# A GNN layer with a routed expert FFN on one core: exact tile counts and the gate's share inside the product in the experts, a 32-bit gate product and constants made earlier in the route

## The reference, cut to what matters

```
x = x + gnn(layernorm(x))            # segment sum over edges, two products, batch norm
h = layernorm(x)
logits = h @ gate_w + gate_b         # (12500, 8)
idx = argmax(softmax(logits)); prb = the softmax at idx
pos = cumsum(one_hot(idx)) of the own expert - 1;  kept = pos < 1954
buf[idx, pos] = h                    # 8 experts x 1954 slots
y = relu(buf @ w1[e] + b1[e]) @ w2[e] + b2[e]      # 256 -> 1024 -> 256
x = x + nan_to_num(y[idx, pos] * prb * kept)
```

## Time and profile before

| | us |
|---|---|
| the profiled execution, device time | 3170.35 |
| its span, first to last instruction | 3168.4 |
| median of the three runs | 3167.32 |
| norm and edge stages in the span | 0 to 2327 |
| route | 2327 to 2543 |
| experts | 2543 to 3168 |

### The profile page before, as it was taken

The page is one execution under the profiler, slowest core; times in us unless marked ns, Lnnn a source line. Parts: engine busy times, 40 slices in busy tenths (PEclk is TensorE's granted clock), DMA queues, the critical chain, the costliest instruction groups (busy, mean ns, idle before and its releaser), DMA issues. The chain is left out here.

```text
span 3168.4 us, 33068 instructions
## 1 busy us (share of the span) xinstructions
PE 1799.3 (57%) x9168; PEld 1062.1 (34%) x9169; DVE 1478.5 (47%) x4301; ACT 693.1 (22%) x1092; POOL 1709.5 (54%) x1690
## 2 busy tenths in 40 slices
PE   0154444455445555554754555564665568989995
PEld 0022222222223222222322222232345445566664
DVE  8765511643225313531252122212348757776885
ACT  6600000000010001000100101010046654636642
POOL 0366664655646565554655344435315556767874
PEclk9976667677767777776777777877766589999997
DMA  7533354334633354343423332212246432222220
GB/s 245 190 104 105 117 183 143 105 89 129 206 96 97 118 195 132 91 127 118 152 85 122 107 123 67 59 50 79 53 144 205 144 94 74 71 86 74 78 83 18
DMA packets 201528, 361.15 MB, mean 114 GB/s; under 512 B 62117, under 2 KB 125947, under 8 KB 201334
## 3 DMA queue, kind: packets, MB, share of 16 engines
q0 software_dynamic: 69152, 185.00, 19.6%
q1 hardware_dynamic: 130038, 172.60, 16.8%
q10 hardware_dynamic: 2144, 1.05, 0.1%
HBM read 291.08 MB, written 71.92 MB: 115 GB/s over the span
## 5 line engine op out<-in xcount | busy, mean ns | idle before, releaser
L773 POOL DMA_INDIRECT halves<-table,halves x1240 | 1186.5, 957 | 1006.4 <-issue 365.6
L850 PE MATMUL e_sums<-halves 128*128 128x256 f16 x1920 | 337.9, 348 | 392.5 <-issue 241.0
L1033 DVE SCALAR_TENSOR_TENSOR nodes<-e_sums,above,nodes 128x256 f32 (+1 forms) x161 | 77.5, 481 | 984.2 <-remote 465.9
L850 PEld LDWEIGHTS e_sums<-halves 128*128 128x128 f16 x1920 | 231.4, 123 | 512.2 <-issue 428.5
L956 ACT ACTIVATE e_hT<-e_up 128x1024 f32<-128x1024 f32 (+1 forms) x25 | 25.1, 1005 | 1511.2 <-remote 1146.8
L1720 POOL TENSOR_TENSOR x_midl<-x_midf,x_midh 128x512 f16<-128x512 f32 x200 | 298.5, 1517 | 103.6 <-ACT x_midh L1854 98.7
L907 PE MATMUL e_up<-e_hT,W1s 128*128 128x512 f32 (+1 forms) x400 | 230.6, 737 | 214.3 <-ACT e_hT L956 117.3
L888 PE MATMUL e_tally<-w1f,counts 128*128 128x512 f16 x490 | 163.1, 477 | 278.9 <-DMA w1f<-table 196.5
L1097 DVE TENSOR_TENSOR counts<-counts,e_tally 128x490 f32 x220 | 160.2, 728 | 243.5 <-PE e_tally L878 124.7
L1810 PE MATMUL x_down<-halves,x_midh 128*128 128x256 f16 x1472 | 251.2, 278 | 19.9 <-DVE x_yb L1947 13.2
L1786 PE MATMUL x_up<-x_xTh,halves 128*128 128x512 f16 (+1 forms) x800 | 231.9, 369 | 3.4 <-ACT x_midh L1854 1.9
(11 more groups left out here) (219 smaller groups left out, 2742.0 us busy)
## 6 DMA issues: line engine op xcount, KB each, us to landing
w1f<-table SPq DMA_DIRECT2D x120, 512.0 KB
halves<-table,halves POOLq DMA_INDIRECT x1240
slot_rows<-halves SPq DMA_DIRECT2D x64, 268.0 KB
x_row<-slot_rows SPq DMA_DIRECT2D x32, 536.0 KB, 7.2
table<-halves SPq DMA_DIRECT2D x25, 512.0 KB, 3.0
counts<-in_x SPq DMA_DIRECT2D x24, 512.0 KB, 5.1
r_xin<-in_x SPq DMA_DIRECT2D x24, 512.0 KB
out<-r_row SPq DMA_DIRECT2D x24, 512.0 KB, 3.3
```

The lines of the kernel that those rows point to most:

```text
L773: pool.indirect_dma_start(got[:, r, t, :], None, table.rearrange("p h d -> (p h) d"), bass.IndirectOffsetOnAxis(ap=idx[:, r, t:t + 1], axi ...
L850: ins = nc.tensor.matmul(sums[:, place, 0:D], hot[:, place, t, :], got[:, r, t, half * D:(half + 1) * D], start=(t == 0 and half == 0), st ...
```

## The change

In the experts: `branch` takes a number of steps, by which `work` gets a tile count. PE has the exact count (1 to 4); ACT's `hidden`, POOL's `low_hidden` and DVE's `finish` have 2 or 4; POOL's `scatter` issues for 2 or 4 tiles. ACT, at the end of `hidden`, writes `b2p` = b2 * prob in four activations of 128x256. DVE has a new function `product` ahead of `finish`: four operations, one per tile, y = down * share + b2p, where `share` = prob * scale is one more small operation in `meta`. They take the place of `yb` and `y`. The memset of `res` covers all of it. PE's `product_down` waits for `product` of the step before.

In the route: `xTh` and `xTl` become one 32-bit `xT`, written by ACT alone; DVE's `low_columns` and the split of the gate's weights go; `gate` is 8 matmuls of 32-bit operands. `seen` is kept for each of the four tiles, so DVE's reduction `more` goes, and `counts` has three matmuls more. The node number in the row is written by ACT in `columns` and no longer by DVE in `route`; POOL waits for it. The four constants are made by POOL at the end of the edge stage, in memory that the edge stage used for zeros.

```diff
@@ stage_edges, at the end of POOL's program
+                pool.wait_ge(s_zeroed, 16 * ZEROS)
+                pool.wait_ge(s_blank, NU * COUNT_ZEROS)
+                nc.gpsimd.memset(fixed.ones[:, :], 1.0).then_inc(s_ones, 1)
+                nc.gpsimd.iota(fixed.rev[:, :], pattern=[[-1, NX]], base=NX, channel_multiplier=0,
+                               allow_small_or_imprecise_dtypes=True)
+                nc.gpsimd.iota(fixed.node1[:, :], pattern=[[P, NB]], base=1, channel_multiplier=1,
+                               allow_small_or_imprecise_dtypes=True)
+                pool.wait_ge(s_ones, 1)
+                nc.gpsimd.affine_select(out=fixed.tri[:, :], in_=fixed.ones[:, :], compare_op=ALU.is_ge, fill=0.0,
+                                        base=0, pattern=[[1, P]], channel_multiplier=-1)
@@ stage_route, tensor
             def gate(q, j, rnd):
-                pe.wait_ge(s_xlo, q + 1)
+                pe.wait_ge(s_xT, q + 1)
                 ...
                 for t in range(QT):
-                    passes = [(x, w, k) for k in range(DK) for x, w in ((xTh, gwh), (xTh, gwl), (xTl, gwh))]
-                    for n, (x, w, k) in enumerate(passes):
-                        ins = nc.tensor.matmul(logit[:, t, :], x[:, k, t * P:(t + 1) * P], w[:, k, :],
-                                               start=(n == 0), stop=(n == len(passes) - 1))
+                    for k in range(DK):
+                        ins = nc.tensor.matmul(logit[:, t, :], xT[:, k, t * P:(t + 1) * P], gw[:, k, :],
+                                               start=(k == 0), stop=(k == DK - 1))
+            def earlier(width, place, last):
+                for t in range(QT):
+                    ins = nc.tensor.matmul(count[:, 0:width, :], ones[:, :],
+                                           seen[:, place, t, :].unsqueeze(1).broadcast_to((P, width, NX)),
+                                           start=(last and t == 0), stop=(last and t == QT - 1))
+                return ins
@@ stage_route, scalar
-                nc.scalar.activation(xTh[:, :, :], back[:, :, :], ACT.Identity, scale=X_SCALE).then_inc(s_xT, 1)
+                nc.scalar.activation(xT[:, :, :], back[:, :, :], ACT.Identity).then_inc(s_xT, 1)
+                nc.scalar.activation(row[:, j, :, D + 2], node1[:, at(q, QT)], ACT.Identity).then_inc(s_col, 1)
@@ stage_route, vector
-            def low_columns(q, j, rnd):
-                dve.wait_ge(s_xT, q + 1)
-                nc.vector.scalar_tensor_tensor(out=xTl[:, :, :], in0=back[:, :, :], scalar=X_SCALE,
-                                               in1=xTh[:, :, :], op0=ALU.mult, op1=ALU.subtract
-                                               ).then_inc(s_xlo, 1)
...
-                picked(q, 7, nc.vector.tensor_reduce(more[:, :], hot[:, :, :].rearrange("p t e -> p e t"), AX.X, ALU.add))
-                picked(q, 7)
-                nc.vector.tensor_tensor(seen[:, (j + 1) % R5, :], seen[:, j, :], more[:, :],
+                nc.vector.tensor_tensor(seen[:, (j + 1) % R5, :, :], seen[:, j, :, :], hot[:, :, :],
                                         ALU.add).then_inc(s_hot, 1)
-            walk(dve, [(low_columns, 3), (add, 1), (route, 3), (norm, 1)], NQ, R5)
+            walk(dve, [(add, 1), (route, 3), (norm, 1)], NQ, R5)
@@ stage_experts
-            def branch(own, j, work, skip, narrow=False):
+            def branch(own, j, work, skip, steps=1):
...
+                def between(low, high):
+                    if high - low == 1:
+                        return work(high * QT // steps) if high else skip()
+                    middle = (low + high) // 2
+                    with engine.If(used > base + middle * QT // steps):
+                        between(middle, high)
+                    with engine.Else():
+                        between(low, middle)
+
+                between(-1, steps)
@@ stage_experts, gpsimd
-                            nc.gpsimd.tensor_tensor(midl[:, j % 2, c, :], midf[:, c % MB, :], midh[:, j % 2, c, :],
+                            nc.gpsimd.tensor_tensor(midl[:, j % 2, c, cols], midf[:, c % MB, cols], midh[:, j % 2, c, cols],
                                                     ALU.subtract).then_inc(s_mlo, 1)
...
-                nc.gpsimd.memset(res[0:16, 0, 0, :], 0.0).then_inc(s_still, 1)
+                nc.gpsimd.memset(res[:, :, :, :], 0.0).then_inc(s_still, 1)
@@ stage_experts, tensor
-                            pe.wait_ge(s_yv, s * 7 - 6)
+                            pe.wait_ge(s_yv, (s - 1) * GUARD + 1)
@@ stage_experts, scalar, at the end of hidden's work
+                        act.wait_ge(s_w, expert(j, rnd) * 64 + 16)
+                        act.wait_ge(s_meta, s * META + META)
+                        if not (isinstance(s, int) and s < 2):
+                            act.wait_ge(s_yv, (s - 2) * GUARD + 1)
+                        for t in range(QT):
+                            ins = nc.scalar.activation(b2p[:, j % 2, t, :], b2s[:, h, :], ACT.Identity,
+                                                       scale=prob[:, j, t:t + 1])
+                        ins.then_inc(s_b2p, 1)
@@ stage_experts, vector
+                def product(s, j, rnd):
+                    def work(tiles):
+                        dve.wait_ge(s_down, s + 1)
+                        dve.wait_ge(s_b2p, s + 1)
+                        ...
+                        for t in range(tiles):
+                            ins = nc.vector.scalar_tensor_tensor(out=y[:, t, :], in0=down[:, t, :], scalar=share[:, j, t:t + 1],
+                                                                 in1=b2p[:, j % 2, t, :], op0=ALU.mult, op1=ALU.add)
+                        ins.then_inc(s_yv, 1)
...
-                        then(1, nc.vector.scalar_tensor_tensor(
-                            out=yb[:, :, :], in0=down[:, :, :], scalar=1.0 / (MID_SCALE * W_SCALE),
-                            in1=b2s[:, j // SG, :].unsqueeze(1).broadcast_to((P, QT, D)), op0=ALU.mult, op1=ALU.add))
-                        then(2, nc.vector.tensor_tensor(y[:, :, :], yb[:, :, :],
-                                                        prob[:, j, :].unsqueeze(2).broadcast_to((P, QT, D)), ALU.mult))
...
-                walk(dve, [(take, 0), (norm, 0), (meta, 0), (split, 4), (finish, 3), (low_columns, 0)], NS, R8)
+                walk(dve, [(take, 0), (norm, 0), (meta, 0), (split, 4), (product, 3), (finish, 3), (low_columns, 0)], NS, R8)
```

More of the change, by code:

```diff
@@ L1356, in counts @@
                 nc.tensor.matmul(count[:, :, :], tri[:, :], hot[:, :, :], start=True, stop=False)
-                nc.tensor.matmul(count[:, :, :], ones[:, :], seen[:, j, :].unsqueeze(1).broadcast_to((P, QT, NX)),
-                                 start=False, stop=False)
+                earlier(QT, j, False)
                 for t in range(QT - 1):
@@ L1363, in counts @@
                 ins.then_inc(s_count, 1)
-            pe.wait_ge(s_gwl, 1)
-            pe.wait_ge(s_tri, 1)
+            pe.wait_ge(s_gw, 32)
             walk(pe, [(turn, 1), (counts, 4), (gate, 3), (turn_back, 2)], NQ, R5)
             pe.wait_ge(s_slot, NQ)
-            nc.tensor.matmul(count[:, 0, :], ones[:, :], seen[:, NQ % R5, :], start=True, stop=True).then_inc(s_count, 1)
+            earlier(1, NQ % R5, True).then_inc(s_count, 1)
         def route_scalar(act):
@@ L1373, in route_scalar @@
             nc.scalar.activation(bns[:, :], bnv[:, :, 1], ACT.Sqrt, bias=epsc[:, 0:1]).then_inc(s_bnsd, 1)
-            act.wait_ge(s_gw, 32)
-            nc.scalar.activation(gwh[:, :, :], gw[:, :, :], ACT.Identity, scale=W_SCALE).then_inc(s_gwh, 1)
             act.wait_ge(s_bn, 2)
@@ L1621, in stage_experts @@
         nodei = sb("x_nodei", [P, RW, QT], I32)
-        yb = sb("x_yb", [P, QT, D], F32)
+        share = sb("x_share", [P, RW, QT], F32)
+        b2p = sb("x_b2p", [P, 2, QT, D], F32)
         y = sb("x_y", [P, QT, D], F32)
@@ L1726, in skip, with work @@
                         pool.sem_inc(s_mlo, FC)
-                    branch(lows, j, work, skip)
+                    branch(lows, j, work, skip, 2)
                 def scatter(s, j, rnd):
-                    def work():
-                        for t in range(QT):
+                    def work(tiles):
+                        for t in range(tiles):
                             pool.indirect_dma_start(
@@ L1794, in skip @@
                         pe.sem_inc(s_up, FC)
-                    branch(ups, j, work, skip, narrow=True)
+                    branch(ups, j, work, skip, QT)
                 def product_down(s, j, rnd):
@@ L1817, in skip @@
                         pe.sem_inc(s_down, 1)
-                    branch(downs, j, work, skip, narrow=True)
+                    branch(downs, j, work, skip, QT)
                 walk(pe, [(take, 0), (turn, 0), (product_up, 1), (product_down, 2)], NS, R8)
@@ L1843, in hidden, with work @@
                     h = j // SG
-                    def work():
+                    def work(tiles):
```

(5 more changed lines are left out.)

140 lines of the change are left out of this document (69 added, 71 removed).

## The result

The kernel after took 3210.6 us in the median of four runs (3195.9 to 3219.9), the kernel before 3172.8 beside it (four runs). The ratio is 1.0127, 95% interval 1.0071 to 1.0183. Forecast was 3133 us, and the range ended at 3165.

The account below looks back on a forecast made before the run. PE was taken to bound full expert steps, DVE the experts' ends, and PE's late release during POOL's burst the route loop. From 3170.35, experts -33 and route -1 gave 3136, or 3133 us against the median 3167.32; range 3098 to 3165.

Parts of the forecast that it names:

- Added: one small operation (0.2 as `share`) and some branch instructions per step, +1.0: Experts, DVE's chain at an expert's end: the added operation and branches cost 1.0 us over the three steps.
- PE's one tile in place of two there gives nothing by itself: Experts, an expert's end: PE's narrower work gains nothing, since PE waits for DVE afterwards.
- Rival 3: Route: the gate's 16 records cost 0.42 us each, PE limits all 25 steps, +70 us, 3203 us; chance 0.07.
- DVE's chain at the ends: Experts, ends like that of expert 0: DVE's chain gets 8.2 us shorter, 24.6 for experts 0, 1 and 6.
- the terms for the halves: Experts' ends: half-wide third finish -3.7 us, `x_xn` beside POOL's narrower subtractions -2.5, one operation beside it -0.8.
- Products: Experts, DVE: four operations of 1.75 us together replace `yb` and `y` at 2.5, -2.2 us over three finishes.
- `b2p`: Experts, ACT: 2.07 us per working step, costed at nothing as hidden during PE's `product_down`; up to 52 us if uncovered.
- Two scatters fewer: Last narrow step, at the kernel's end: two scatters fewer at 0.97 + 0.30 us each, -2.6 us.
- Wide memset: Experts, POOL: the wider memset of `res` runs before the first subtraction while PE transposes; nothing, at most 2 us.
- Route: Route stage as a whole: -1 us, between -17 and +25, with the 32-bit gate costing 0 in the loop.
- the reading that the burst holds PE's release up: Route loop: PE's release is late during POOL's burst of four scatters; `r_lg` starts 1.98 us after the fourth begins.
- rival 1: Route: releases follow the gate, the row add's landing limits, -15 us, 3118 us; chance 0.18.

Follow-up runs that it names:

- e2: The kernel before with the experts stage of after, so only the experts' edits; 1.0156 of before, experts 654.5 us.
- e3: The kernel after with PE's two products in two widths (2 and 4 tiles) in place of four; 0.9896 of before, experts 593.3 us.
- e4: The kernel before with two more arms per PE product that repeat the same work, nothing computed differently; 1.0349 of before, experts 708.3 us.
- e10: The kernel after with PE's second product as four guarded one-tile blocks, the first still in four arms; 0.9979 of before, experts 615.6 us.
- e11: The kernel after with two widths for PE's first product only, the second keeping four arms; 1.0009 of before, experts 627.0 us.
- e5: e3 with the half-wide arms of ACT, POOL and DVE in the experts taken away; 0.9975 of before, experts 621.5 us.
- e9: e7 with `yb` and `y` back in place of `share`, `b2p` and the four products; 0.9890 of before, experts 587.6 us.
- e7: The kernel after with PE's first product in two widths, second in guarded one-tile blocks, narrow steps' scatters halved, `res` memset narrow; 0.9856 of before, experts 585.8 us.
- e1: The kernel after with the experts stage of before, so only route and edge edits; 0.9969 of before, experts 613.7 us.

## Why the prediction was wrong, point by point

- **The step that failed** is the last of the list on DVE's chain: "Added: one small operation (0.2 as `share`) and some branch instructions per step, +1.0", together with "PE's one tile in place of two there gives nothing by itself". Branches were counted by the instructions executed. What costs is the length of the program that they enclose: 61 us of experts (e2 against e3) where the step had 1.0 at each of three ends. No rival had this mechanism. Rival 3 named 3203 us, near the measured time, for a reason that did not occur, and that is no hit.
- The kernel before had the sign of it: 4.05 us at 2843.49 put down to 'issue', and 110 instruction packets on its page. A row of the DMA table with a share of 0.2% was passed over because it is small; its cost is not bandwidth but that PE stands still.
- The Trainium skill (Runtime: NRT & Kernel Launch, Instruction fetch mechanics) says that fetching ahead is purely sequential and that a taken branch to a page not yet in the engine's window "forces a DMA fetch of the target page before execution can continue". e4 agrees, with 87 us for nothing but dead arms; e10 and e11 add that it is not all or nothing. The rule speaks against this change and should have been a rival.
- **DVE's chain at the ends** was right in its main term: e3 against e5 gives 28 us for the halves, where the terms for the halves (-3.7, -2.5, -0.8 at three ends, and the kernel's end) come to some 25. At the end of expert 0 the chain from the first finish to the end of the last `x_xn` takes 42.6 us in e3 (1990.98 to 2033.62) against 48.6, so 6.0 less, forecast 8.2. The first `x_xn`, put at -2.5, fell from 3.90 to 2.21; the last, beside POOL, stayed at 4.71. PE's idle time there falls to 3.69 + 1.51 + 1.85 = 7.05 us and not to 2.
- **Products**: 476 ns each, forecast 0.44, and four in 1.65 us. Yet the saving of 7 us is not there; they lose about 4 (e5, e9). **`b2p`**, costed at nothing, is a second term that failed: ACT's busy share of full steps was taken for its cover, but at an expert's end ACT also has the split, and `x_ex` came late (1.92 us in e3).
- **Two scatters fewer**, -2.6, was misread: the branch of the scatters has no half width, so `scatter` issues four in every filled step and not 2 or 4 as "The change" says, and both kernels issue 100. e7 does what the step assumed.
- **Wide memset**, "nothing, at most 2": 3.51 us on POOL at the moment of the first `x_xn`, which takes 4.64 in place of 1.44 us: +3.2. The cover named, PE's transposes, waits for just that `x_xn`. With the narrow memset in e7 PE starts 1.5 us after `x_xn` again.
- **Route**, -1 forecast, 0 measured on that chip. A gate record costs 3.56 / 16 = 0.22 us, forecast 0.21, and hides beside the scatters. But in the step shown `r_lg` starts 0.65 us after the gate's end and 0.5 after the fourth scatter began, not 1.98. That step is one kind of several: of 23 starts of `r_lg` ten lie 1.9 to 2.1 us behind the last scatter's, nine lie 0.3 to 1.2 behind it, and the steps take 5 to 11.5 us and not an even 7.6. So the reading that the burst holds PE's release up is not a rule of the loop; what sets a step was not taken apart. The waits of the row add for landings grew as rival 1 had it, from 3 (3.6 us) to 11 (15.4 us), and the route still took 193.9 us, not 15 less.

With PE's arms at e3's level the ratio is 0.9896, and 0.989 was forecast. That is partly luck. The experts of e3 are 20 us shorter than e1's, forecast 33 (bounds 18 and 45), and the route's edits gave 0.3%, some 8 us, forecast 1. The 28 us in all are 1.1% of a run of 2572 us; of 3167 they would be 0.9%. The direction and the largest term were right, the smaller ones were too favourable, and the one left at 1 us outweighed them all. In the chances 0.28 + 0.18 is 0.46 and not 0.48; nothing rests on it.

## What to carry to other kernels

Before an engine's work is specialised by size, count the instructions of all arms, not those executed: here each packet of some 250 more cost 0.7 to 1.6 us of the stage's time; between 55 and 66 packets no difference was seen. Specialise where arms are short (ACT, POOL and DVE: six to twenty instructions, 28 us gained), and on PE share the code by guarded blocks of one tile. On a page, read the instruction queues beside the waits by 'issue' and PEq; a packet count that rises while the engine's busy time stays the same is the sign.

## What the runs showed of the hardware

- The edge stage, the same program, ends near 1750 us on one kind of chip and 2330 on another, while the experts differ by 1 to 2%. Ratios between kernels carried over: e1 times e2 gives 1.0125, where the first pair has 1.0127.
